# Two attention products on halves of the TensorE array: value product on column halves, scores on row halves

## The reference, cut to what matters

```python
q, k = rotary_xpos(l2norm(q) * qs, l2norm(k) * ksc)
sim = jnp.einsum('bhwid,bhwjd->bhwij', bq * 8, bk)   # 128 queries x 256 keys (the window before and this one)
attn = jax.nn.softmax(jnp.where(mask, -big, sim), axis=-1)
out = jnp.einsum('bhwij,bhwjd->bhwid', attn, bv)     # 128 x 64 per head
x = x + out.transpose(...).reshape(b, n, 512) @ wo
```

## Time and profile before

| | us |
|---|---|
| runs, median of 3 | 3162.67 |
| profiled execution | 3164.78 |
| its span | 3162.5 |
| TensorE matmul busy | 3041.8 (96%) |
| VectorE busy | 2242.3 (71%) |
| ScalarE busy | 2327.7 (74%) |
| GpSimd busy | 1561.3 (49%) |
| mean granted TensorE clock | 0.983 |

### The profile page before, as it was taken

One profiled execution on the slowest core, in us unless ns is written; L12 is line 12 of the kernel. 1 busy time (PEld: TensorE's weight loads), 2 busy tenths in 40 slices (PEclk: granted clock), 3 DMA queues, 4 the chain that ended last, 5 costly groups with the idle time before them and its releaser, 6 DMA issues.

```text
span 3162.5 us, 67715 instructions
## 1 busy us (share of the span) xinstructions
PE 3041.8 (96%) x22436; PEld 2870.2 (91%) x22436; DVE 2242.3 (71%) x6843; ACT 2327.7 (74%) x5301; POOL 1561.3 (49%) x1524
## 2 busy tenths in 40 slices
PE   7999748999999999999999999999999999999998
PEld 6888637899999999999999899999999999999998
DVE  3989956777777777777777567766666767666663
ACT  5989836777777777777777677777777777777774
POOL 2323134555555555555555455555555555555543
PEclk9999969999999999999999999999999999999999
DMA  2242034444444444544444545444444444444441
GB/s 91 65 171 77 28 98 112 116 113 117 109 102 115 105 108 110 117 108 105 113 107 96 135 118 159 110 104 104 104 109 109 110 109 104 105 104 106 111 103 34
DMA packets 262511, 333.57 MB, mean 105 GB/s; under 512 B 40978, under 2 KB 159508, under 8 KB 261140
## 3 DMA queue, kind: packets, MB, share of 16 engines
q1 hardware_dynamic: 262164, 329.25, 42.3%
HBM read 77.33 MB, written 42.05 MB: 38 GB/s over the span
## 4 chain that ended last, share of the span: by engine, by line
PE 90%; DVE 3%; SPq 2%; issue 2%; DMA 1%; ACT 1%; POOL 1%; DVEq 0%; POOLq 0%; ACTq 0%
PE ps L393 45%; PE ps L475 13%; PE ps L367 9%; PE ps L461 7%; PE ps L449 4%; PE ps L450 4%; PE ps L436 3%; PE ps L484 2%; SPq L1468 1%; PE ps L413 1%; PE ps L502 1%; PE ps L354 0%; PE ps L539 0%; PE ps L538 0%; DVE Sm L1060 0%
## 5 line engine op out<-in xcount | busy, mean ns | idle before, releaser
L740 ACT ACTIVATE Sm<-Sm,nb,sc 128x256 f32<-128x256 f32 (+1 forms) x1024 | 597.6, 588 | 0.8
L1060 DVE CUSTOM_DVE_ANT_0 Sm<-ps,mask 128x256 f32<-128x256 f32 (+1 forms) x1024 | 369.0, 417 | 169.6 <-PE ps L450 167.5
L475 PE MATMUL ps<-vv,PT 128*128 128x64 f32 x4032 | 478.4, 272 | 0.0
L475 PEld LDWEIGHTS ps<-vv,PT 128*128 128x128 f32 x4032 | 470.4, 192 | 0.0
L393 PE MATMUL ps<-zTh,W1h 128*128 128x256 f32 (+1 forms) x1408 | 409.1, 291 | 0.0
L718 ACT ACTIVATE sq<-ps 128x512 f32<-128x512 f32 x256 | 152.9, 597 | 348.0 <-PE ps L393 348.0
L1133 DVE SCALAR_TENSOR_TENSOR Gl<-ps,vecs,Gl 128x256 f32<-128x256 f32 (+1 forms) x384 | 173.4, 479 | 330.3 <-PE ps L393 284.8
L393 PE MATMUL ps<-zTl,W1h 128*128 128x256 f32 (+1 forms) x1408 | 397.2, 282 | 0.0
L393 PE MATMUL ps<-zTh,W1l 128*128 128x256 f32 (+1 forms) x1408 | 391.7, 278 | 0.0
L1206 POOL TENSOR_TENSOR rs<-rs,mhalf 128x16 f32<-128x16 f32 x128 | 372.3, 2908 | 0.0
L1292 POOL TENSOR_TENSOR uTl<-Gl,uTh 128x512 fp32r<-128x512 f32 (+1 forms) x192 | 212.8, 1108 | 322.0 <-ACT uTh L789 184.8
(11 more groups left out here) (184 smaller groups left out, 8806.6 us busy)
## 6 DMA issues: line engine op xcount, KB each, us to landing
kkh<-kh SPq DMA_DIRECT2D x512, 128.0 KB, 2.4
kkl<-kl SPq DMA_DIRECT2D x512, 128.0 KB, 2.4
qq<-qTh SPq DMA_DIRECT2D x256, 128.0 KB, 2.4
qq<-qTl SPq DMA_DIRECT2D x256, 128.0 KB, 2.4
tb<-tab SPq DMA_DIRECT2D x128, 128.0 KB, 2.5
xc<-x SPq DMA_DIRECT2D x32, 256.0 KB, 3.0
rwkv_scratch<-rw SPq DMA_DIRECT2D x32, 256.0 KB, 2.6
rk<-rwkv_scratch SPq DMA_DIRECT2D x64, 128.0 KB, 2.6
```

The source lines that it names most:

```text
L475: ins = pe.matmul(PS[:, k, 64 * i:64 * i + 64], PT[:, h, s * 128:(s + 1) * 128], vv[:, v, h, :], start=s == sides[0], stop=s == sides[-1])
L740: act.activation(Sm[:, h, c0:c1_], Sm[:, h, c0:c1_], ACT.Exp, bias=nb[:, h:h + 1], scale=sc[:, n % 4, h:h + 1], accum_out=sm[:, n % 2, h:h ...
L1060: dve.tensor_tensor_reduce(Sm[:, h, c0:c1_], PS[:, bank["scores", n, q, h % 2], (h // 2 % 2) * 256 + c0:(h // 2 % 2) * 256 + c1_], mask[:, ...
```

## The change

1. `scores`: the operands are used where `qk_hi` and `qk_lo` write them: heads 2c and 2c+1 on partitions 0 to 63 and 64 to 127. Each head takes three fp32r matmuls with 64 rows instead of two with 128 (24 a window). They are issued in pairs, one on the upper, one on the lower half of the rows, into two banks. `scores(n, 0)` and `scores(n, 1)` now stand together, ahead of `qkv(t-2, 1)`. The 12 stacking DMAs and their waits go.
2. `pv`: the operands change places: `vv` (128x64) is stationary and 128 columns of `PT` move. The even head writes partitions 0 to 63 and the odd head 64 to 127 of one bank, in pairs. Both calls stand together near the start of the step, right after `turn_r`. The result comes out turned: features on partitions.
3. The softmax sums must therefore be turned instead: one reciprocal for 8 heads (`o_sums`), a copy of each value to 64 columns on GpSimd (`spread`), 4 transposes (`turn_r`), a copy out of PSUM on ScalarE (`rT_out`), and the product with the value product's bank on VectorE (`o_norm`). `oT_hi` and `oT_lo` split from SBUF.
4. The pipeline is one step shorter: `wo_mm` and all behind it come one step earlier, STEPS2 = U + 13.

```diff
+    if live(6):
+        yield "rT", t - 6
+        yield "pv", t - 6
     if live(7):
+        yield "wo", t - 7
...
     if live(4):
         yield "scores", t - 4, 0, 0
         yield "scores", t - 4, 0, 1
+        yield "scores", t - 4, 1, 0
+        yield "scores", t - 4, 1, 1
     if live(2):
         yield "qkv", t - 2, 1
-    if live(4):
-        yield "scores", t - 4, 1, 0
-        yield "scores", t - 4, 1, 1
...
             def scores(n, q):
-                w.wait_ge(S[f"stk1{n % 2}"], STACKED[1] * (n // 2 + 1))
-                w.wait_ge(S[f"stk0{n % 2}"], STACKED[0] * (n // 2 + 1))
-                for h in range(4 * q, 4 * q + 4):
...
-                    pe.matmul(dst, qq[:, h % 2, c, :], kkh[:, side, h % 2, c, :], start=True, stop=False)
-                    ins = pe.matmul(dst, qq[:, h % 2, c, :], kkl[:, side, h % 2, c, :], start=False, stop=True)
+                w.wait_ge(S["qkh"], 2 * n + 2)
+                w.wait_ge(S["qkl"], 2 * n + 2)
+                for par in range(2):
+                    w.wait_ge(*read_out(former["scores", n, q, par]))
+                for c in (2 * q, 2 * q + 1):
+                    for i, (a, b) in enumerate(((0, 0), (1, 0), (0, 1))):
+                        for par in range(2):
+                            rows = slice(64 * par, 64 * par + 64)
+                            ins = pe.matmul(PS[:, bank["scores", n, q, par], (c % 2) * 256 + c0:(c % 2) * 256 + c1_],
+                                            qT[a][rows, c, :], kT[b][rows, side, c, :], start=i == 0, stop=i == 2)
...
             def pv(n, q):
-                        ins = pe.matmul(PS[:, k, 64 * i:64 * i + 64], PT[:, h, s * 128:(s + 1) * 128], vv[:, v, h, :],
-                                        start=s == sides[0], stop=s == sides[-1])
+                        for par in range(2):
+                            ins = pe.matmul(PS[64 * par:64 * par + 64, k, c * 128:(c + 1) * 128], vv[:, v, 2 * c + par, :],
+                                            PT[:, 2 * c + par, s * 128:(s + 1) * 128],
+                                            start=s == sides[0], stop=s == sides[-1])
...
+            def turn_r(n):
+                k = bank["rT", n]
+                w.wait_ge(S["rob"], n + 1)
+                w.wait_ge(*read_out(former["rT", n]))
+                for c in range(4):
+                    ins = pe.transpose(PS[:, k, c * 128:(c + 1) * 128],
+                                       rob[:, 2 * c:2 * c + 2, :].rearrange("p h d -> p (h d)"), ident[:, :])
...
+            def rT_out(n):
+                w.wait_ge(S["p7"], n + 1)
+                w.wait_ge(S["oTl"], n)
+                act.activation(flat(oF[:, :, :]), PS[:, bank["rT", n], :], ACT.Copy).then_inc(S["rT"], 1)
...
+            def o_sums(n):
+                w.wait_ge(S["ex"], 8 * n + 8)
+                w.wait_ge(S["rob"], n)
+                dve.reciprocal(ro[:, :], sm[:, n % 2, :]).then_inc(S["ro"], 1)
+
+            def o_norm(n):
+                w.wait_ge(S["p6"], 2 * n + 2)
+                w.wait_ge(S["rT"], n + 1)
+                dve.tensor_tensor(flat(oF[:, :, :]), PS[:, bank["pv", n], :], flat(oF[:, :, :]),
+                                  ALU.mult).then_inc(S["on"], 1)
...
+            def spread(n):
+                w.wait_ge(S["ro"], n + 1)
+                w.wait_ge(S["p7"], n)
+                pool.tensor_copy(rob[:, :, :], ro[:, :].unsqueeze(2).broadcast_to([128, 8, 64])).then_inc(S["rob"], 1)
```

More of the change, by code:

```diff
@@ L59 @@
 STEPS1 = NCH + 5
-STEPS2 = U + 14
+STEPS2 = U + 13
 PK, PV, PR, PT1 = 0, 2, 4, 6
@@ L544, in live @@
                     return 0 <= t - d < U
-                odd = t % 2
-                if live(8):
-                    wo_mm(t - 8)
-                if live(7):
[L550 to L558, removed]
+                odd = 1 - t % 2
+                if live(6):
+                    turn_r(t - 6)
+                    pv(t - 6, 0)
+                    pv(t - 6, 1)
+                if live(7):
+                    wo_mm(t - 7)
+                if live(10) and not odd:
+                    turn_z(t - 10)
+                if live(11) and odd:
+                    mlp((t - 11) // 2, 0)
+                if live(12) and not odd:
+                    w2_mm(t - 13)
                 if live(5):
@@ L561, in tensor_program @@
                     turn_p(t - 5, 1)
[L562 to L567, removed]
+                if live(11) and odd:
+                    mlp((t - 11) // 2, 1)
+                if live(12) and not odd:
+                    w2_mm(t - 12)
                 if live(5):
@@ L570, in tensor_program @@
                     turn_p(t - 5, 3)
-                if live(12) and odd:
-                    mlp((t - 12) // 2, 2)
+                if live(11) and odd:
+                    mlp((t - 11) // 2, 2)
                 if live(4):
                     scores(t - 4, 0)
+                    scores(t - 4, 1)
                 if live(2):
                     qkv(t - 2, 1)
-                if live(4):
-                    scores(t - 4, 1)
                 if live(3):
@@ L588, in tensor_program @@
                     turn_h(t - 1)
-                if live(11) and odd:
-                    turn_z(t - 11)
+                if live(10) and odd:
+                    turn_z(t - 10)
                 if live(0) and t < NG:
@@ L794, in live @@
                     return 0 <= t - d < U
-                odd = t % 2
-                if live(7):
-                    oT_hi(t - 7)
+                odd = 1 - t % 2
+                if live(6):
+                    rT_out(t - 6)
                 if live(5):
                     exp(t - 5, 1)
[L801 to L804, removed]
+                if live(10) and not odd:
+                    z_out(t - 10)
+                if live(11) and odd:
+                    gelu((t - 11) // 2, 0)
                 if live(5):
@@ L807, in scalar_program @@
                     p_out(t - 5, 1)
-                if live(12) and odd:
-                    u_hi((t - 12) // 2, 0)
-                    gelu((t - 12) // 2, 1)
+                if live(11) and odd:
+                    u_hi((t - 11) // 2, 0)
+                    gelu((t - 11) // 2, 1)
                 if live(5):
@@ L834, in scalar_program @@
                     hT_hi(t - 1)
-                if live(11) and odd:
-                    z_out(t - 11)
+                if live(10) and odd:
+                    z_out(t - 10)
         def vector_program(dve):
@@ L1180, in vector_program @@
                     masked_max(t - 4, 1)
-                if live(12) and odd:
-                    u_tail((t - 12) // 2)
+                if live(11) and odd:
+                    u_tail((t - 11) // 2)
+                if live(6):
+                    oT_lo(t - 6)
+                if live(5):
+                    o_sums(t - 5)
                 if live(2):
@@ L1349, in gpsimd_program @@
                     table(t - 1)
-                if live(11) and odd:
-                    zT_lo(t - 11)
+                if live(10) and odd:
+                    zT_lo(t - 10)
                 if live(0) and t < NG:
```

209 lines of the change are left out of this document (79 added, 130 removed).

## The result

The changed kernel takes 2961.59 us (median of 4, 2958.53 to 2962.41) against 3162.85 for the kernel before, run beside it: ratio 0.936, 95% interval 0.9344 to 0.9376, so 201 us less. 3010 was forecast, and a range of 2920 to 3165.

The account below looks back on a forecast made before the run. TensorE's instruction stream was taken as the bound. Value product, scores and mode changes gave -1.2 us a window, -1.1 with slack, x 128 = -141; with -12 for fill, 3164.8 became 3012, as a median 3010 us; range 2920 to 3165.

Parts of the forecast that it names:

- likeliest case: On TensorE: matmuls on different array halves run side by side, about 3010 us; chance 0.50.
- Value product: `pv` on TensorE: column halves side by side take 1.73 us a window for 3.41, so -1.7.
- Scores: Scores on TensorE: row halves in pairs take 1.43 us for 1.91, -0.48, offset by +0.5 for changes of mode.
- Rival B: Scores on TensorE: row halves load in turn, 2.57 us (+0.66), 0.0 a window in all, 3150 us; chance 0.17.
- Entering and leaving: TensorE's four changes a window between whole array and halves: 0.25 us each (between 0.16 and 0.35), 1.0 a window.
- Tight places: Two places where other engines' work barely precedes TensorE's need; 0.1 us a window added for any that don't hold.
- (a): Bank ring, step after an `mlp` step, layer 2: VectorE frees the bank before `rT` needs it, by 0.3 us.
- (b): ScalarE's last exponentials end at T0 + 15.9 (T0: scores' start), ahead of `turn_p(2)` at T0 + 16.7, by 0.8 us.
- C: Rival: ScalarE or VectorE sets the step at a tight place, 0.6 us a window more, 3085 us; chance 0.12.
- Fill, -12: Pipeline ends: 10 of 15.5 us of waits for the stacking DMAs go, one step less counts 2; ends 0 and -20.
- SyncE's waits: SyncE's own waits, 568 us for the scores alone, hold nobody on the path in the steady part.
- Rival A: On TensorE: array halves take turns, value product stays 3.46 us, scores +0.95, about 3405 us; chance 0.13.

Follow-up runs that it names:

- e3: Changed kernel with the value product's two calls split, the output projection (`wo_mm`) between them: 3017.07 us.
- e4: Changed kernel with the scores split into two blocks, the projection `qkv(t-2, 1)` between them: 3050.01 us.
- e9: Changed kernel with only ScalarE's order changed: second half of the exponentials behind `v_out` in the same step, not at the next step's start: 3037.09 us.
- e11: Changed kernel with the value product directly ahead of the scores, a second `PT` buffer and the normalising moved along, ScalarE's order kept: 3040.65 us.
- e1: Changed kernel with the value product's loop order changed: per call all even heads' matmuls, then all odd heads', instead of pairs: 3032.32 us.
- e2: Changed kernel with the scores' loop order changed: per call six matmuls of row half 0, then six of half 1, instead of pairs: 3001.07 us.
- e5: Changed kernel with all 16 value product matmuls (one call for two) of column half 0 ahead of all 16 of half 1: 3123.46 us.
- e6b: Changed kernel with the old scores back (stacked 128-row operands, 12 DMAs a window), `NY` 7 for 8: 3050.44 us.
- e7: Changed kernel with the value product directly behind the scores, one step earlier, three changes of mode for four: 3332.74 us.
- e10: Changed kernel with the value product directly ahead of the scores, a second `PT` buffer, normalising moved along, and e9's exponentials order: 3126.35 us.

## Why the prediction was right, and where not

The direction and the likeliest case were right: the halves run side by side.

- *Value product*, -1.7: the moving measures 1.73 for 3.41, as worked out. What I left out is that each old block ended 0.085 us late (a float32 block of 64 columns into an fp32r one), which the change removed as well: -0.17 a window.
- *Scores*, -0.48 + 0.5: the moving measures 1.43 as said. Rival B, loads of row halves in turn, is shown wrong by the pairs 0.12 us apart, each with two loads of 128 columns.
- *Entering and leaving*: the mis-sized term. I took 1.0 us a window for four changes; they are 0.36 + 0.39 = 0.75, 0.17 to 0.2 each, just above my floor of 0.16: 32 us too much. My 0.35 put a wait for the last matmul's end (0.16) and a whole load (0.19) one behind the other. The loads show the first part in about that size and not the second: the first load of the scores begins 0.20 after the last matmul before it started, 0.19 late, and its matmul starts 0.01 behind it. The whole error, by the profiled executions' own times (3164.8 to 2961.1, -204, for -153): 32 of the changes, 22 of the old blocks' ends, 13 of the tight places, less 11 of the fill and 5 of rounding and of the four windows with half the records. The Trainium skill, "TensorEngine Tiling (Array Packing)", Key Properties, has two rules on this, and both agree with the record: a change of mode is paid (0.17 to 0.2 us, which the page does not size), and tiles load and multiply in parallel (pairs 0.12 us apart).
- *Tight places*: (a) and (b) both held; TensorE has 0.4 us without work in 600, so the 0.1 us a window that I added was not needed. But e3, e4, e9 and e11 show how little there was: in each, TensorE waits for VectorE's rotation, by up to 0.8 to 1.5 us a time. C was wrong for this change; in nine of the twelve edits (all but e1, e2 and e5) TensorE did wait for another engine or its DMAs in the steady part. One reading of (b) was 0.1 off: the last exponentials end at 2363.20 by their row, not 2363.10, so the margin was 0.7.
- *Fill, -12*: wrong. The waits for the stacking went, and waits for GpSimd's `Ar` and `rob` took their place; the net is -0.9. In a fill the next engine in the chain was nearly as late as the one removed.
- *SyncE's waits "hold nobody on the path in the steady part"*: true of the kernel before, and of no use as a statement on the change. e6b shows that with the value product's part alone, in the order that the changed kernel has, the 12 DMAs cost 67 us of waits. The two halves of the change are worth -112 (value product alone: 3162.9 to 3050.4) and -89 (the scores' part on top), where my sum gave the scores about nothing and the value product -1.2 x 128 = -154. The sum of both came out near because TensorE's own time is all that is left when both are in.
- *Steps of layer 1*: 17.74 and 21.53 us measured between `turn_r` starts, 18.3 and 21.7 forecast.
- *Rival A* was ruled out for pairs, and e5 shows what it looks like: with each half's matmuls in one run, the value product takes 28.5 slots and the changes (3.25 us), of A's 32 slots.

## What to carry to other kernels

Alternate between the halves matmul by matmul: that is the order in which all of them ran side by side here, where runs of 6, 8 and 16 records on one half lost 3, 5.6 and 12.5 slots. Price each change of mode at 0.2 us and put all halves work in as few blocks as the other engines allow. Before splitting a change into parts by cost, ask for each part what chain it would leave exposed once the other part is in: most of the worth of the scores' part was in the DMAs it removed. When one engine is at work for 99.9% of the steady part, other engines' orders are not free to edit: a microsecond of order on ScalarE (e9) was 75 us.

## What the runs showed of the hardware that I had not expected

- Matmuls on different halves leave program order. e2 starts half 0's seventh ahead of half 1's fifth and sixth, and e1 and e5 fit a half that holds three to four records. The Trainium skill, "TensorE: Matmul & The Clock Gate", Part 3, says that matmuls on tiles start and end strictly in program order; this record differs, and the measurement decides. With halves taken in turn, as in the changed kernel, the two can't be told apart.
- A change from row halves to column halves costs as much as one to the whole array (e7: 0.21 against 0.21 behind the last pair), not two, and so does the way from column to row halves (e10).
- A weight load of 64 float32 columns on a column half has a mean of 139 ns in the record, where the old value product's 128 columns have 192: not half, and still hidden, since the two loads of a pair run side by side, 7 ns apart. The columns alone don't set the record's length: the loads of 128 columns for the float32 transposes have 141 ns in the same trace.
- A change of mode delays the weight load: the first of the scores begins 0.31 us behind the load before it, where loads within the block follow each other after 0.12.
